# A transformer layer with sixteen routed experts on one Trainium2 core: expert tiles in pairs, rows that carry weight and destination, finished tiles scattered to their tokens

## The reference

```python
x = L0_attn_x                                   # (8, 512, 256), f32
x = x + layernorm(attention(layernorm(x)))      # 16 heads of 16
x = x + layernorm(ffn(layernorm(x)))
# ffn, per token t (T = 4096 tokens, E = 16 experts, hidden 128, D = 256, S = 512):
shared  = (silu(x @ sfc1.T) * (x @ sfc2.T)) @ sfc3.T
logits  = x @ gate_w.T;  the two largest are taken, softmax over the two -> weights
moe[t]  = sum over the token's two experts e of  weight * (silu(x[t] @ w1[e].T) @ w2[e].T)
result  = moe + shared
```

## Time and profile before

| | |
|---|---|
| median of 3 runs | 1055.41 us |
| the profiled execution's own time / its span | 1056.11 / 1054.4 us |
| PE, DVE, ACT, POOL busy over the span | 80%, 65%, 56%, 34% |
| block 3, from the first scatter's issue | 704 to 798 us |
| block 4 | 805 (first matmul) to 936 us |
| block 5 | 937 to 1054 us |

### The profile page before, as it was taken

The page is one execution under the profiler, slowest core; times in us unless marked ns, Lnnn a source line. Parts: engine busy times, 40 slices in busy tenths (PEclk is TensorE's granted clock), DMA queues, the critical chain, the costliest instruction groups (busy, mean ns, idle before and its releaser), DMA issues. The chain is left out here.

```text
span 1054.4 us, 16887 instructions
## 1 busy us (share of the span) xinstructions
PE 847.4 (80%) x4978; PEld 537.3 (51%) x4979; DVE 681.3 (65%) x1338; ACT 593.7 (56%) x1271; POOL 356.5 (34%) x431
## 2 busy tenths in 40 slices
PE   4469999999999999999856777339954999969771
PEld 3234444444444444433326666228843888758661
DVE  4477777778877787788515888563322666627775
ACT  2117777676777767777745765213322777744442
POOL 4350604225060513300004444126671111135873
PEclk9569999999999999999987777559986999979895
DMA  7776547284656636171011211002222555432443
GB/s 134 172 168 138 105 111 172 71 165 104 155 93 129 134 102 121 42 132 32 2 48 42 70 40 43 3 25 90 85 97 94 179 170 168 149 97 74 127 127 115
DMA packets 69667, 108.79 MB, mean 103 GB/s; under 512 B 9827, under 2 KB 39011, under 8 KB 69603
## 3 DMA queue, kind: packets, MB, share of 16 engines
q1 hardware_dynamic: 60578, 80.72, 33.3%
q0 software_dynamic: 9024, 27.27, 7.8%
HBM read 55.53 MB, written 50.33 MB: 100 GB/s over the span
## 5 line engine op out<-in xcount | busy, mean ns | idle before, releaser
L407 DVE TENSOR_REDUCE negmax<-ring 128x2 f32<-128x1024 f32 x256 | 309.5, 1220 | 90.2 <-PE ring L554 88.0
L362 ACT ACTIVATE probs<-score 128x512 f32<-128x512 f32 x512 | 278.7, 599 | 82.2 <-PE score L566 82.2
L566 PE MATMUL score<-q_st,k_st 64*128 64x512 f32 x512 | 209.8, 469 | 13.1 <-ACT probs L362 8.7
L554 PE MATMUL ring<-k_st,q_st 48*128 48x512 f32 x512 | 181.4, 457 | 9.0 <-DMA k_st<-turned 5.2
L566 PEld LDWEIGHTS score<-q_st,k_st 64*128 64x128 f32 x512 | 83.7, 184 | 152.9 <-ACT probs L362 99.2
L578 PE MATMUL av<-probs,v_aug 128*32 128x512 f32 x1024 | 136.4, 604 | 2.6 <-ACT probs L362 1.2
L274 POOL CAST part_r<-negmax 128x16 fp32r<-128x16 f32 x32 | 6.3, 197 | 302.4 <-DVE negmax L407 302.4
L1236 POOL DMA_INDIRECT rows_in<-O,slots_i x64 | 64.0, 1000 | 60.0 <-DVE slots_i L1222 33.1
L1329 DVE TENSOR_TENSOR m_xlo<-m_bx,m_xhi 128x256 fp32r<-128x256 f32 x80 | 34.0, 425 | 73.2 <-ACT m_xhi L1310 73.2
L554 PEld LDWEIGHTS ring<-k_st,q_st 48*128 48x128 f32 x512 | 69.9, 188 | 14.3 <-issue 7.9
L1422 POOL DMA_INDIRECT e_picked<-rows_out,slots_i x64 | 66.3, 1035 | 24.0 <-issue 16.7
(11 more groups left out here) (214 smaller groups left out, 1911.3 us busy)
## 6 DMA issues: line engine op xcount, KB each, us to landing
q_st<-turned SPq DMA_DIRECT2D x96, 128.0 KB, 4.2
k_st<-turned SPq DMA_DIRECT2D x96, 128.0 KB, 5.4
rows_in<-zero SPq DMA_DIRECT2D x20, 512.0 KB, 5.2
m_rows<-rows_in SPq DMA_DIRECT2D x40, 256.0 KB, 2.7
rows_out<-m_y POOLq DMA_DIRECT2D x20, 512.0 KB, 3.4
X<-in_x SPq DMA_DIRECT2D x8, 512.0 KB, 9.9
turned<-turned_hiq SPq DMA_DIRECT2D x16, 256.0 KB, 2.8
turned<-turned_loq SPq DMA_DIRECT2D x16, 256.0 KB, 2.5
```

The lines of the kernel that those rows point to most:

```text
L362: nc.scalar.activation(probs[r // 2 % 2][r % 2][:, a, :], score[:, a, :], ACT.Exp, scale=HD ** -0.5).then_inc(exp_done, 1)
L407: nc.vector.tensor_reduce(negmax[Gn % 2][:, t, 2 * p:2 * p + 2], ring[t % 2][:, :, :], AX.X, ALU.max, negate=True).then_inc(max_done, 1)
L554: last = nc.tensor.matmul(half[:, a, :], q[rows, t * P:(t + 1) * P], k[rows, :], start=True, stop=True)
L566: nc.tensor.matmul(score[:, a, :], k[rows, kt * P:(kt + 1) * P], q[rows, :], start=True, stop=True).then_inc(sc_ps, 1)
```

## The change

- `rows_in` becomes `rows_wide`, whose rows are 258 words (`ROW = D + 2`): the 256 values, the row's weight, and its destination as an integer. Padding rows carry weight 0 and a destination from `PADS` (8192) on. `O` gets the same width (`O_rows`), its two extra words filled by one DVE copy and one POOL iota; for the second choice SP copies two tiles and their extra words into `second_rows` (2 buffers), and POOL scatters from there. The fills of block 1 write 258 words per row; `turned` moves into the freed old tensor.
- Block 4 works on 40 pairs of tiles, written out without loops, with 10 load buffers of a pair, 4 output buffers of a pair, and registers loaded 16 at a time. In step s, PE transposes pair s+1, then turns the hidden rows of s-2, then multiplies s with w1 and s-3 with w2; ACT casts s+1, casts `m_ghi` of s-2, takes SiLU of s-1 and copies out s-4 in two instructions; DVE does `m_xlo` of s+1, `m_glo` of s-2, `m_pre` of s. ACT multiplies a tile by its rows' weights as it copies it out. POOL scatters each tile by the destinations in its rows, to token order; destinations over `PADS - 1` are dropped by the bounds check. The block doesn't wait for the last scatters to land; SP waits for them at the start of block 5.
- Block 5 is written out. SP loads the two expert results of every batch row with 16 plain DMAs of 512 KB into SBUF where the expert weights lay; POOL adds the two (two instructions of 128 x 512 per batch row), DVE adds the sum to `O` (two of 128 x 512). PE transposes `O` directly. The shared expert's 16 hidden parts (4 batch rows by 4 parts) are numbered m = 16 to 31; the expert rows of batch rows 0 to 6 are added at m = 18, 20 ... 30 (`SLOT`), those of batch row 7 after the last part.

```diff
+ROW = D + 2
+PADS = 2 * B * N
@@ attention @@
-                sp.dma_start(fill[G], zero[:, :].unsqueeze(1).broadcast_to([P, fill.shape[2], D])).then_inc(filled, 16)
+                sp.dma_start(fill[G], pad[:, :].unsqueeze(1).broadcast_to([P, fill.shape[2], ROW])).then_inc(filled, 16)
@@ block 3, sync @@
+            sp.wait_ge(extras_set, 4)
+            for h in range(NT // 2):
+                if h > 1:
+                    sp.wait_ge(scattered[h % 2], 32 * (h // 2))
+                sp.dma_start(second_rows[h % 2][:, :, 0:D], O[:, 2 * h:2 * h + 2, :]).then_inc(copied[h % 2], 16)
+                sp.dma_start(second_rows[h % 2][:, :, D:ROW], extra[:, 2 * h:2 * h + 2, :]).then_inc(copied[h % 2], 16)
@@ block 3, vector, ahead of the chain @@
+            nc.vector.tensor_copy(O_rows[:, :, D], wts[:, :, 0]).then_inc(extras_set, 1)
+            nc.vector.tensor_copy(extra[:, :, 0], wts[:, :, 1]).then_inc(extras_set, 1)
@@ block 3, gpsimd @@
+            for h in range(NT // 2):
+                for t in (2 * h, 2 * h + 1):
+                    nc.gpsimd.indirect_dma_start(out=rows_in, out_offset=bass.IndirectOffsetOnAxis(ap=slots_i[:, t, 0:1], axis=0),
+                                                 in_=O_rows[:, t, :], in_offset=None).then_inc(row_s, 16)
+                pool.wait_ge(copied[h % 2], 32 * (h // 2 + 1))
+                for t in range(2):
+                    nc.gpsimd.indirect_dma_start(out=rows_in, out_offset=bass.IndirectOffsetOnAxis(ap=slots_i[:, 2 * h + t, 1:2], axis=0),
+                                                 in_=second_rows[h % 2][:, t, :], in_offset=None).then_inc(scattered[h % 2], 16)
...
@@ block 4, gpsimd @@
+            for s in range(PAIRS):
+                for f in range(2):
+                    pool.wait_ge(kept_s, 2 * s + f + 1)
+                    nc.gpsimd.indirect_dma_start(
+                        out=rows_out, out_offset=bass.IndirectOffsetOnAxis(ap=rows[s % LOADS][:, f, D + 1:ROW].bitcast(U32), axis=0),
+                        in_=y[s % HELD][:, f, :], in_offset=None, bounds_check=PADS - 1, oob_is_err=False).then_inc(sent[s % LOADS], 16)
@@ block 5 @@
+            for i in range(LOADS):
+                sp.wait_ge(sent[i], 32 * (PAIRS // LOADS))
             for b in range(B):
+                for k in range(2):
+                    sp.dma_start(picked[:, b, k, :, :], moe_v[k, b]).then_inc(loaded[b], 16)
+        SLOT = {HALF * SC + 2 * b + 2: b for b in range(B - 1)}
...
+                    both = (picked[:, b, k, 2 * h:2 * h + 2, :] for k in range(2))
+                    nc.gpsimd.tensor_tensor(y[2 * (b % 2) + h][:, :, :], *both, ALU.add).then_inc(pair_s, 1)
...
+            pair_sum(0)
+            pair_sum(1)
+            for b in range(B):
+                row_scale(b)
+                if b + 2 < B:
+                    pair_sum(b + 2)
...
+            for m in range(HALF * SC, B * SC):
+                r, n = m // SC, m % SC
+                multiply(m)
+                if m - 1 in SLOT:
+                    scale_of_mean(SLOT[m - 1])
+                if m in SLOT:
+                    whole(SLOT[m])
+                hidden_low(m)
+                if n == SC - 1 and r + 1 < B:
+                    low(r + 1)
+                if m in SLOT:
+                    statistics(SLOT[m])
+                if m - 2 in SLOT:
+                    residual(SLOT[m - 2])
+            whole(B - 1)
+            statistics(B - 1)
+            residual(B - 2)
+            scale_of_mean(B - 1)
+            residual(B - 1)
```

More of the change, by code:

```diff
@@ L14 @@
 F32R = mybir.dt.float32r
+U32 = mybir.dt.uint32
 ALU = mybir.AluOpType
@@ L1272, in valid @@
-        def valid(s):
-            return not isinstance(s, int) or 0 <= s < TILES
-        in_v = rows_in.rearrange("(n f p) d -> n p f d", f=2, p=P)
-        out_v = rows_out.rearrange("(n f p) d -> n p f d", f=4, p=P)
-        def sync(sp):
-            def load(two, j, round_):
-                if later(round_):
-                    sp.wait_ge(xt_s, (two - 3) * 2)
-                sp.dma_start(rows[j][:, :, :], in_v[bass.ds(two, 1)].rearrange("a p f d -> p (a f) d")).then_inc(load_s[j], 16)
-            for j in range(4):
-                load(j, j, 0)
-            with sp.Fori(1, TILES // 8) as eight:
-                for j in range(4):
-                    load(eight * 4 + j, j, eight)
@@ new lines, in feed_forward @@
+        tr_s, hi_s, lo_s, a_s, g_s, silu_s, h_s, hh_s, hl_s, y_s, kept_s = shared_counts
+        pair_s, sum_s, bn_s, ag_s, var_s, pow_s, nmr_s, z_s, res_s, out_s = (
+            sub.enter_context(nc.semaphore("e_" + x)) for x in "pair sum bn ag var pow nmr z res out".split())
+        two = lambda name, shape, dt=F32: [sbt(f"{name}{i}", shape, dt) for i in range(2)]
+        t_hi, t_lo = sbt("t_hi", [P, DC, N], F32R), sbt("t_lo", [P, DC, N], F32R)
+        silu, h_hi, h_lo = two("silu", [P, N]), two("h_hi", [P, N], F32R), two("h_lo", [P, N], F32R)
@@ L1450, in scalar @@
-            shared.copy_row(act, 0)
-            shared.high(act, 0)
-            shared_rows(act, pair)
-            shared.keep(act, HALF - 1)
-            normalise(B - 2)
+                    nc.scalar.activation(O[:, b * QT + t, :], O[:, b * QT + t, :], ACT.Identity,
+                                         bias=nmr[b % 2][:, t:t + 1], scale=rstd[b % 2][:, t:t + 1]).then_inc(z_s, 1)
+            high(HALF)
+            for m in range(HALF * SC, B * SC):
+                r, n = m // SC, m % SC
+                silus(m)
+                if n == 0 and r > HALF:
+                    keep(r - 1)
+                if n == SC - 1 and r + 1 < B:
+                    high(r + 1)
+                if m - 1 in SLOT:
+                    normalise(SLOT[m - 1])
@@ L1540, in vector, with tensor, transposes, first @@
             residual(B - 1)
+        def tensor(pe):
+            def transposes(r):
+                pe.wait_ge(lo_s, r * DC)
+                for c in range(DC):
+                    for t in range(QT):
+                        last = nc.tensor.transpose(bank_t[c][:, t * P:(t + 1) * P], O[:, r * QT + t, c * P:(c + 1) * P], ident[:, :])
+                    last.then_inc(tr_s, 1)
+            def first(m):
+                n = m % SC
+                turned = [(t_hi[:, c, :], t_lo[:, c, :]) for c in range(DC)]
+                pe.wait_ge(silu_s, m - 1)
+                three(bank_a[m % 2][:, :], [(weight(S1 + c * S + n * P, P), turned[c]) for c in range(DC)]).then_inc(a_s, 1)
+                pe.wait_ge(h_s, m - 1)
+                three(bank_g[m % 2][:, :], [(weight(S2 + c * S + n * P, P), turned[c]) for c in range(DC)]).then_inc(g_s, 1)
+            def second(m):
+                r, n = m // SC, m % SC
+                pe.wait_ge(hl_s, m + 1)
+                if n == 0:
+                    pe.wait_ge(kept_s, r * 2)
+                for t in range(QT):
+                    hidden = [h[m % 2][:, t * P:(t + 1) * P] for h in (h_hi, h_lo)]
+                    last = three_acc(bank_y[t // 2][:, (t % 2) * D:(t % 2 + 1) * D], hidden, weight(S3 + n * D, D),
+                                     n == 0 and t % 2 == 0, n == SC - 1)
+                last.then_inc(y_s, 1)
+            transposes(HALF)
+            for r in range(HALF, B):
+                pe.wait_ge(lo_s, r * DC + DC)
+                first(r * SC)
+                for n in range(1, SC):
+                    first(r * SC + n)
+                    if n == SC - 1 and r + 1 < B:
+                        transposes(r + 1)
+                    second(r * SC + n - 1)
+                second(r * SC + SC - 1)
         run_block(nc, sync=sync, gpsimd=gpsimd, scalar=scalar, vector=vector, tensor=tensor)
```

473 lines of the change are left out of this document (222 added, 251 removed).

## The result

The changed kernel takes **1048.53 us** (median of 9 runs, 1046.93 to 1053.45) against 1058.43 for the kernel before on the same chips (9 runs, 1053.79 to 1059.86): a ratio of 0.9914, 95% interval 0.9898 to 0.9931. It is faster, but by 10 us and not by 38: 1017.3 was forecast, 1004 to 1044 given as the range. The profiled execution took 1047.89 us, its span is 1046.1.

The account below looks back on a forecast made before the run. POOL was taken to bound blocks 3 and 4, in block 4 by little; +0.4 ahead of block 3's chain, -19.1 in block 4 and -19.4 in block 5 took 1055.4 to 1017.3 us, range 1004 to 1044.

Parts of the forecast that it names:

- rival 5: Block 3: copies landing in 5.9 instead of 2.5 us make the last rounds late, +6, up to +34; chance 0.07.
- the circle of the earlier trace: Block 4 before: DVE and ACT wait on each other in turn, 1.40 us per tile; the change was to open it.
- rival 4: Block 4: a circle remains, pairs go no faster than two tiles, 2.80 us, +11.5, 1029 us; chance 0.13.
- rivals 2 and 3: Block 4 scatters dearer: 1.36 us each, +32, 1049, chance 0.15; or from 1.44 us on, slower than before, chance 0.03.
- The tail: End of block 5: two copies, two adds, handoffs, then statistics to the end as before, 14.1 us.
- signs of being wrong: Scatters over 1.1 us, POOL waiting for ACT in block 4, PE waiting on h_lo all through block 5, changed attention.
- +4, between 0 and 16: Block 5: POOL's adds and DVE's two-operand work overlap by chance, costing 4 us in all, between 0 and 16.
- The 74.8 us: Block 5: the shared expert's time, taken from block 3, where it ran without this load.
- Rival 1: Block 5: exclusive port, each of POOL's 16 adds holds up DVE by 1.28 us, +20.5 instead of +4, 1034; chance 0.12.
- The second step: End of block 4: last scatter to block 5, 5.55 us before, at most 3.1 without the landing wait, taken as 2.1.
- the pitch in block 4: Block 4: POOL's scatters, one per tile, start 1.26 us apart and set the block's length.
- the ramp: Start of block 4: the first output comes after five steps of 2.4 us, 12.0 us.

Follow-up runs that it names:

- the moves: Changed kernel with each later pair_sum held until the following part's h_lo, and the residual one part later behind h_lo: 1034.0 us, ratio 0.9774.
- the cut of the statistics: Kernel with blocks 4 and 5 joined, adds held and residual later, plus bn_aggr and the eps sum behind the next product: 1079.0 us, ratio 0.9982.
- Plain stores: Changed kernel, but SP stores block 4's pairs in the order made, one plain transfer each, POOL idle there: 1026.3 us, ratio 0.9693.
- one transfer landed long before: Kernel with SP's plain stores in block 4, plus a single 128 KB POOL transfer at that block's start: 1042.2 us, ratio 0.9638.
- Joining the blocks: Changed kernel, but each engine passes from block 4 to block 5 by itself, without all engines meeting: 1034.8 us, ratio 0.978.
- holding the adds: Changed kernel, but POOL holds each later pair_sum until DVE is through the following part's h_lo: 1041.3 us, ratio 0.9838.

## Why the prediction was wrong

**Right:** the order of the engines. POOL bounds block 4 at its pitch without a gap; it never waits for SP's copies in block 3 (rival 5 is out: the rounds of 8.2 us do fit into 10.1); the circle of the earlier trace rows is open, most pairs 2.3 us apart where POOL doesn't hold them (rival 4 out); the bounds check is cheap (rivals 2 and 3 out, on these chips). The tail is 13.3 us, 14.1 worked out. Of the signs of being wrong, one came: PE waits for `h_lo` all through block 5.

**The step that failed** is block 5's "+4, between 0 and 16", together with the 74.8 us that it was added to. I counted how long two engines use the port (5.1 and 7.8 of 18.7 us) and let them overlap *by chance*. They don't meet by chance. POOL's power is released by `e_vareps`, and the residual stands right behind `e_vareps` on DVE; `e_nmr` is released by the power, and `pair_sum` stands right behind the power on POOL. A release starts both sides of a meeting at the same instant, in 7 of 8 powers and 6 of 8 `e_nmr` (the others have no residual or no add to meet), and in the slots always ahead of the instruction for which PE waits. The runs with the moves put a price on it: 13.3 us of the stage (114.1 to 100.8), 8.3 as shorter waits of PE and 5 as PE's clock. And the length was counted by the wrong partner: an `e_nmr` of 0.16 us grows to 1.23 because it waits out a whole add. Rival 1 had this rule, with each add holding up DVE by its full 1.28; it gave 1034, but on the wrong instructions, since most adds met nothing that mattered, and the powers, which I had left out of the port's account, did. I gave it 0.12, because "POOL is idle three quarters of the time", which is an average and says nothing of two instructions that one event starts.

The 74.8 us were block 3's, at a granted clock of 0.96, while the earlier trace rows had 0.90 for this stage. PE is busy for 83.3 us in the last stage now; in block 3 it was for 73.6, and the first eight transposes, which the earlier trace rows leaves out, are 1.9 here. So about 8 of the 17.8 us are PE working slower, a term that the sum put at nothing. They go with the long wait ahead of the block and the three long waits in it. The waits for `h_lo` are 16.2 us, against the 4 of the sum and 0.8 in block 3, which makes 11; the tail gives about 1 back.

The 4.5 us that are left with both moves: I had found 16.3 us of DVE work for 18.7 and called it tight. It is not even: a part with a slot holds 4.6 us (0.68, 2 x 0.65, 0.68, 1.40, 0.38, 0.17) for 4.2 of PE, the time from one `h_lo` to the next in block 3. Of the waits that are left three times 0.87 us are again a meeting, that of the two pairs of adds; how much the fullness of DVE costs by itself no run shows, since the cut of the statistics brought a meeting back.

**The second step** is the end of block 4: "of which the landing is at least 2.4; it is no longer waited for, so at most 3.1 stay". I read the 5.55 us of the earlier trace rows as landing plus something small. Plain stores show 0.8 us with nothing of POOL's in the block, one transfer landed long before shows the same, and scatters to the block's end show 6.9, of which landing is some 1.2. So about 5 us are neither landing nor the change of blocks as such, and what they are stays open. But it was in view in the kernel before, in the change from block 3 to 4. The last scatter starts at 794.23 and lands in 2.4 us, at about 796.6; the first load of block 4, from the timeline:

```profile
802.27 8.12 SPq L1282 DMA_DIRECT2D m_rows<-rows_in  x6
```

It is issued 7.1 us after that scatter's end and 5.6 after its landing. I read only the change that the edit touched.

**Sizes:** the pitch in block 4 is 1.29 for 1.26 (+2.4), the ramp 13.6 for 12.0 (+1.6). One thing was missed altogether, though it is no error of the sum: PE had stood for 18.25 us when block 5 began, since ACT's lead of four pairs is time in which only POOL runs. Joining the blocks let PE start 15.3 us earlier, and 13.7 of them came through.

**The range** ended at 1044. It held either error, the 17.8 of block 5 or the 8.8 of block 4's three rows, and just the two together (1043.9), but not the 3.3 of the rows ahead of them besides. The bound of 16 for block 5 was itself too small, since it counted adds and no powers, and no clock.

## What to carry to other kernels

Work out a shared port by who releases whom, not by busy shares: here two instructions released by one event met each time that both were there, and a short one paid for a whole long one. Put the work that can wait behind the instruction that another engine waits for, then a meeting costs little; here holding the adds gave 7.2 of the 10.2 us that removing them gave. Look at PE's granted clock before carrying a time from one stage to another, and after each long wait: over a third of the two moves' gain was clock. And an engine that runs behind a buffer of finished tiles should not be met by all others at a block's end: let each go on by itself.

## What was not expected of the hardware

**Issuing a scatter waits for a two-operand DVE instruction.** In the changed kernel's block 3, seven of the 63 scatters after the first take 1.23 to 1.39 us instead of 0.96, and each of the seven starts within 0.3 us of the start of an `h_lo`, whose two operands are both in SBUF (timeline, both engines):

```profile
774.98 1.35 POOL L1260 DMA_INDIRECT rows_wide<-second_rows,slots_i  x1 [0.30 <-issue]
779.15 1.39 POOL L1256 DMA_INDIRECT rows_wide<-O,slots_i  x1 [0.30 <-issue]
774.81 0.69 DVE L1082 TENSOR_TENSOR s_shared_h_lo<-s_shared_silu,s_shared_h_hi 128x512 fp32r<-128x512 f32 x1 [0.69 <-ACT s_shared_h_hi L1060]
779.02 0.69 DVE L1082 TENSOR_TENSOR s_shared_h_lo<-s_shared_silu,s_shared_h_hi 128x512 fp32r<-128x512 f32 x1 [0.69 <-ACT s_shared_h_hi L1060]
```

The product of SiLU and gate (L1078), with one operand in PSUM, has no such scatter beside it. The Trainium skill (SBUF — State Buffer, section Who interferes with whom) has the exclusion that `e_nmr` shows (0.16 to 1.23), and infers that issuing descriptors is left alone by a plain two-operand instruction; these seven speak against the inference. They end 0.83 us after the `h_lo` does, and cost 2.5 us together.

**A block's end costs more when POOL scatters up to it**: 0.8 us after no transfer of POOL's and 0.83 after one landed long before, 6.9 after 80 scatters, though these land within 1.2 us of the last one's end. **PE's clock falls after a long wait**: to 0.50 at the three waits of 3.45 to 3.66 us and not at waits of 1.2 to 1.4, in the changed kernel's last stage; with both moves at one of three waits of 2.35. **The same kernel's gain can change sign with the chip**: 0.9914 and 1.0199, with the stages of the table above.
